# A cross-attention kernel: output rows on GpSimd, a two-operation end of the normalisation, weight folds from pieces, three loads on ScalarE's queue, new orders

## The chip, the cores and the metric

The kernel runs on one core of one Trainium2 chip. The metric is device time in microseconds (us), the median of several executions. The engines are TensorE (PE; PEld is its weight load), VectorE (DVE), ScalarE (ACT), GpSimd (POOL) and SyncE (SP), which here only issues transfers. Each engine works through its own instructions in order.

## What is computed

Sixteen batches (`B`), each with 100 query rows (`L`) and 361 context rows (`S`) of 512 features (`H`). A grouped attention layer with 32 query heads over 8 key heads of 16 features, residual and normalisation, and then a second, single-headed attention over the same context:

```python
q = hidden_state @ Wq + bq            # 32 heads, 4 per key head
k = encoder_hidden_state @ Wk + bk    # 8 heads
v = encoder_hidden_state @ Wv + bv
scores = jnp.einsum('bkgld,bksd->bkgls', q, k) * scale + mask
attn = jax.nn.softmax(scores, axis=-1)
out = jnp.einsum('bkgls,bksd->bkgld', attn, v)      # -> (B, L, H)
x = out @ Wo + bo + hidden_state
x1 = (x - mu) * jax.lax.rsqrt(var + EPS) * gamma + beta

q, k, v = x1 @ w_q.T, ctx @ w_k.T, ctx @ w_v.T
probs = jax.nn.softmax(q @ k.T / sqrt(512), axis=-1)
return x1 + alpha * (probs @ v) @ w_o.T
```

## The kernel before

Everything is fp32; products that need it are split in a high part (`_h`) and a low part (`_l`) and done as three fast products, in `product` (L505 to L507 of the profile). The second layer's four weights are folded once at the start into two 512x512 matrices, `fold_m` (w_q and w_k, 16 products, L669) and `fold_n` (w_v and w_o, L682).

A batch goes through these steps. Transposed x and context (`xT`, `cT`) are loaded and split: ScalarE writes the high part (`x_high`, `c_high`), GpSimd the low one (`x_low` L2333, `c_low` L2339). TensorE makes q, k and v. q and k go through DRAM (`queries_out`, `keys_out`, `stacks_in`) to be stacked, 96 rows deep. `heads` (L543) then makes the scores of each of the 32 heads once with the queries as rows; VectorE takes their row maxima (`maxima`, L1439). The maxima are turned, split (`maxima_high`, `maxima_low`) and written by `maxima_in` (L217) as rows 96 and 97 of the stack `qs`, for each half of the heads. `scores` (L526 for the first chunk of the keys, L530 and L531 for two more) makes the scores again, with keys as rows and the maxima subtracted. VectorE adds the mask to chunk 0 (L1425), ScalarE copies chunks 1 and 2 (`copy_scores`, L1912), GpSimd adds the mask there (`add_mask`, L2327), ScalarE takes the exponential (`probabilities`, L1918), TensorE multiplies by v (`values`, L559), each product with the sum of its row beside it.

Then comes the output path. `output` copies a half's rows to `o_s`, `rows_out` writes them to DRAM. `sums_in` (L232) and `rows_in` (L240) read back sums and rows; VectorE's `reciprocals` (L1477) inverts the sums; they go through DRAM (`reciprocals_out` L245, `reciprocals_in` L254) into `r_b`, spread over the rows. VectorE's `normalize` (L1482) multiplies, ScalarE's `o_high` (L2006) writes the high part, VectorE's `o_low` (L1486) the low one. `y_part` multiplies by Wo. `y_sum` adds the residual, to which GpSimd has added the bias (`residual_bias`, L2355); `y_stats`, `y_moments` (L1520) give mean and variance, GpSimd's `variance` and `deviation` (L2344, L2350) the reciprocal deviation, and VectorE ends the normalisation in three operations: `centre` (L1525, needs the deviation), `gain` (L1534), `shift` (L1539). `turn_x1` (L572) turns the result, and the second layer follows: `xm_part`, `turn_xm`, `s1_part` (L659), softmax, `turn_p1`, `cx_part` (L616), `d_part` (L626), `residual` (L1505), `result_out`. It needs the context twice more: `late_keys_in` (cT_s) and `ctx_in` (ctx_n).

The order of each engine's work is written out by hand, call by call: batches 0 to 3 and 12 to 15 singly, 4 to 12 by a loop over `i` on every engine. In turn `i`, TensorE does the later heads of batch `i` and the first of `i + 1`, the scores and values of `i - 1` and `i`, the q, k and v of `i + 1` and `i + 2`, and the second layer of `i - 2`, interleaved in small pieces. A wait stops all that its engine has behind it; that goes for SyncE's queue, which issues every transfer, too.

Of the kernel before, what the change touches and what calls it, by code (L numbers as in the profile page):

```python
# [14 lines left out]
P = 128  # L15
# [21 lines left out]
def build(nc, xT_d, x_d, ctxT_d, ctx_d, mask_d, maskT_d, wq_d, wk_d, wv_d, wo_d, bq_d, bk_d, bv_d,  # L37
          bo_d, gamma_d, beta_d, w1q_d, w1k_d, w1v_d, w1o_d, alpha_d, out_d):
    with ExitStack() as ctx:
# [3 lines left out]
        def sem(name):  # L43
# [71 lines left out]
        w_q, w_k, w_v, w_b, w_1, w_s, w_o, w_2 = (sem(n) for n in ("w_q", "w_k", "w_v", "w_b", "w_1", "w_s", "w_o", "w_2"))  # L115
        wh_ok, wl_ok, zero_ok, half_ok, bvb_ok = (sem(n) for n in ("wh_ok", "wl_ok", "zero_ok", "half_ok", "bvb_ok"))
# [19 lines left out]
        y_mm, y_ok, st_ok, mv_ok, ve_ok, rstd_ok, xc_ok, xg_ok, x1_ok = (  # L136
            sem(n) for n in ("y_mm", "y_ok", "st_ok", "mv_ok", "ve_ok", "rstd_ok", "xc_ok", "xg_ok", "x1_ok"))
# [10 lines left out]
        def _(sp):  # L148
# [26 lines left out]
            def weights_o():  # L175
                sp.wait_ge(wh_ok, 1)
                sp.wait_ge(wl_ok, 1)
                sp.dma_start(n_w[:, :, :].rearrange("p a b -> p (a b)"), wo_d).then_inc(w_o, 16)
# [9 lines left out]

            def ctx_turned_in(b):
                wait(sp, ch_ok, b)  # L190
                wait(sp, cl_ok, b)
                sp.dma_start(cT[:, :], ctxT_d[b, :, :]).then_inc(c_in, 16)
# [63 lines left out]
            def residual_in(b):  # L256
                wait(sp, xg_ok, b)
                sp.dma_start(y[:, :], x_d[b, :, :]).then_inc(xn_in, 16)

            def late_keys_in(b):  # L260
                if b == 0:
                    sp.wait_ge(g_mm, 4)
                wait(sp, l_mm, b)
                sp.dma_start(cT_s, ctxT_d[b, :, :]).then_inc(c4_in, 16)

            def ctx_in(b):
                if b == 0:
                    sp.wait_ge(g_mm, 4)
                wait(sp, cx_mm, b)
                sp.dma_start(ctx_n, ctx_d[b, :, :, :]).then_inc(cn_in, 16)  # L270
# [36 lines left out]
            fold_m_in()  # L307
            weights_v()
            weights_k()
            weights_q()  # L310
            mask_in(0)
            biases()
            x_turned_in(0)
            residual_in(0)
            mask_in(1)
            norm_in()
            ctx_turned_in(0)
            x_turned_in(1)
            weights_o()
            fold_n_in()  # L320
            queries_out(0)
            keys_out(0)
            ctx_turned_in(1)
            stacks_in(0, 0, 0, 2)
            stacks_in(0, 0, 2, 4)
            x_turned_in(2)
            stacks_in(0, 1, 0, 2)
            mask_turned_in(0)
            stacks_in(0, 1, 2, 4)
            mask_turned_in(1)  # L330
            queries_out(1)
            ctx_turned_in(2)
# [5 lines left out]
            x_turned_in(3)  # L338
# [3 lines left out]
            ctx_turned_in(3)  # L342
            rows_out(0, 0)
            queries_out(2)
            keys_out(2)
# [5 lines left out]
            x_turned_in(4)  # L351
            maxima_in(1, 1)
            rows_in(0)
            sums_in(0)
            mask_turned_in(2)
            stacks_in(2, 1, 2, 4)
            reciprocals_out(0)
            reciprocals_in(0)
            ctx_in(0)
            queries_out(3)  # L360
            rows_out(1, 0)
            maxima_in(2, 0)
            mask_in(3)
            keys_out(3)
            late_keys_in(0)
# [3 lines left out]
            ctx_turned_in(4)  # L369
            maxima_in(2, 1)  # L370
            rows_in(1)
            sums_in(1)
            x_turned_in(5)
            stacks_in(3, 1, 0, 2)
            reciprocals_out(1)
            residual_in(1)
            stacks_in(3, 1, 2, 4)
            mask_turned_in(3)
            reciprocals_in(1)
            rows_out(2, 0)  # L380
            mask_in(4)
            ctx_in(1)
            late_keys_in(1)
            queries_out(4)
            maxima_in(3, 0)
            keys_out(4)
            stacks_in(4, 0, 0, 2)
            stacks_in(4, 0, 2, 4)
            rows_out(2, 1)
            ctx_turned_in(5)  # L390
            result_out(0)
            maxima_in(3, 1)
            rows_in(2)
            sums_in(2)
            residual_in(2)

            for i in range(4, 13):
                stacks_in(i, 1, 0, 2)
                reciprocals_out(i - 2)
                stacks_in(i, 1, 2, 4)  # L400
                mask_turned_in(i)
                mask_in(i + 1)
                reciprocals_in(i - 2)
                late_keys_in(i - 2)
# [3 lines left out]
                x_turned_in(i + 2)  # L408
                rows_out(i - 1, 0)
                stacks_in(i + 1, 0, 0, 2)  # L410
                stacks_in(i + 1, 0, 2, 4)
                rows_out(i - 1, 1)
                ctx_turned_in(i + 2)
                sums_in(i - 1)
                ctx_in(i - 2)
                rows_in(i - 1)
                maxima_in(i, 1)
                residual_in(i - 1)
                result_out(i - 3)

            x_turned_in(15)
            reciprocals_out(11)
            late_keys_in(11)
            mask_turned_in(13)
            reciprocals_in(11)
            stacks_in(13, 1, 0, 2)
            stacks_in(13, 1, 2, 4)
            queries_out(14)
            ctx_turned_in(15)
            maxima_in(13, 0)  # L430
            keys_out(14)
            mask_in(14)
            rows_out(12, 0)
            stacks_in(14, 0, 0, 2)
            stacks_in(14, 0, 2, 4)
            rows_out(12, 1)
            stacks_in(14, 1, 0, 2)
            sums_in(12)
            maxima_in(13, 1)
            result_out(10)  # L440
            ctx_in(11)
            rows_in(12)
            reciprocals_out(12)
            residual_in(12)
# [2089 lines left out]
```

## Time and profile before

| what | value |
|---|---|
| median of 3 runs | 739.95 us (734.6 to 741.24) |
| the profiled execution, its own time | 737.84 us |
| its span | 736.1 us |
| TensorE busy | 669.4 us, 91% |
| VectorE busy | 512.7 us, 70% |
| ScalarE busy | 393.5 us, 53% |
| GpSimd busy | 369.4 us, 50% |
| mean granted TensorE clock | 0.972 |
| transfers | 110.51 MB, mean 150 GB/s |

The span is the time from first to last instruction in the profile, and some 1.7 us less than the time that is measured. A busy share of a matmul includes its pipeline, so TensorE at 91% is nearer its limit than the number says. The chain that ended last lies on TensorE for 49% of the span and on transfers for 23%. In the 40 slices of the page, TensorE is at 9 or 8 tenths from the second slice to the 35th.

### The profile page before, as it was taken

How to read it: one execution, taken by the hardware profiler on the slowest of the kernel's cores; microseconds unless marked ns; L12 is line 12 of the kernel's file. 1: busy time of each engine (PE TensorE's matmuls, PEld its weight loads, DVE VectorE, ACT ScalarE, POOL GpSimd, SP SyncE). 2: the span in 40 equal slices, each digit the busy share in tenths (PEclk: the TensorE clock that was granted, in tenths of full speed). 3: DMA queues.
4: the chain of work that ended last, by engine and by line, in shares of the span. 5: the costliest groups of instructions: out<-in, count | busy, mean ns of one | idle time of the engine just before them, and what ended most of it. 6: DMA issues, size and time to landing. Idle time of an engine off the chain costs nothing.

```text
span 736.1 us, 11738 instructions
## 1 busy us (share of the span) xinstructions
PE 669.4 (91%) x3658; PEld 462.2 (63%) x3658; DVE 512.7 (70%) x1467; ACT 393.5 (53%) x589; POOL 369.4 (50%) x225
## 2 busy tenths in 40 slices
PE   5998998989999999999989999999999989897756
PEld 2556656666676767776758677676767656563434
DVE  1258879778696869786857778696978778754120
ACT  2324766645566656666655656475666636564100
POOL 3454766545556564646455565556555534554000
PEclk9999999999999999999999999999999989999987
DMA  7696685755768685858493758678687644541500
GB/s 285 254 145 132 158 128 174 148 155 133 151 148 202 139 188 118 219 124 196 134 194 116 195 127 205 144 172 177 134 198 160 140 141 82 97 151 47 170 9 12
DMA packets 60856, 110.51 MB, mean 150 GB/s; under 512 B 11661, under 2 KB 50125, under 8 KB 60026
## 3 DMA queue, kind: packets, MB, share of 16 engines
q1 hardware_dynamic: 60794, 109.76, 63.2%
q8 instruction: 30, 0.49, 0.3%
q14 instruction: 32, 0.26, 0.2%
HBM read 86.79 MB, written 22.52 MB: 149 GB/s over the span
## 4 chain that ended last, share of the span: by engine, by line
PE 49%; DMA 23%; DVE 9%; issue 8%; SPq 7%; POOL 2%; ACT 1%; POOLq 0%; DVEq 0%; ACTq 0%
PE mx_ps L543 7%; PE work L505 6%; PE work L507 5%; PE work L506 5%; DMA qs<-mt_l 5%; PE work L626 5%; PE o_ps L559 5%; DMA late<-r_dr 4%; DMA r_dr<-rden 4%; DMA o_dr<-o_s 3%; PE work L616 3%; DMA k_dr<-k_l 3%; DVE mx_ps L1439 2%; DVE late L1482 2%; PE sc_ps L526 2%
## 5 line engine op out<-in xcount | busy, mean ns | idle before, releaser
L1439 DVE CUSTOM_DVE_ANT_0 mx_ps<-mx_ps,mask_n 100x361 f32<-100x361 f32 x512 | 270.2, 544 | 90.7 <-PE mx_ps L543 87.9
L2327 POOL TENSOR_TENSOR pr<-pr,mask_t 128x800 f32<-128x800 f32 x128 | 249.5, 1962 | 162.8 <-ACT pr L1912 162.6
L543 PE MATMUL mx_ps<-ks,qs 96*100 96x362 f32 x512 | 182.9, 379 | 12.9 <-DVE mx L1439 9.7
L1912 ACT ACTIVATE pr<-sc_ps 128x800 f32<-128x800 f32 x128 | 106.9, 835 | 106.1 <-PE sc_ps L531 59.7
L1918 ACT ACTIVATE pr<-pr 128x1200 f32<-128x1200 f32 x128 | 152.1, 1203 | 12.0 <-POOL pr L2327 7.2
L543 PEld LDWEIGHTS mx_ps<-ks,qs 96*100 96x100 f32 x512 | 85.2, 168 | 50.5 <-DVE mx L1439 25.8
L1425 DVE TENSOR_TENSOR pr<-sc_ps,mask_t 128x400 f32<-128x400 f32 x128 | 73.0, 571 | 17.5 <-PE sc_ps L526 10.6
L559 PE MATMUL o_ps<-pr,va 128*32 128x400 f32 (+1 forms) x768 | 72.7, 512 | 3.4 <-ACT pr L1918 3.4
L1439 DVE DVE_READ_ACCUMULATOR2_ANT mx<- 100x1 f32 x512 | 72.1, 141 | 0.0
L626 PE MATMUL work<-n_w,late 128*100 128x512 f32 x128 | 69.4, 635 | 1.5 <-ACT late L1984 1.4
L2339 POOL TENSOR_TENSOR c_l<-cT,c_h 128x1448 fp32r<-128x1448 f32 x16 | 53.6, 3350 | 29.7 <-ACT c_h L1939 29.7
L526 PE MATMUL sc_ps<-qs,ks 98*128 98x400 f32 x128 | 56.8, 444 | 11.1 <-DMA qs<-mt_l 10.9
L616 PEld LDWEIGHTS work<-late 128*128 128x128 f32 (+1 forms) x384 | 53.1, 199 | 3.9 <-ACT late L1979 1.6
L530 PE MATMUL sc_ps<-qs,ks 98*128 98x400 f32 x128 | 52.2, 408 | 3.1 <-ACT pr L1912 3.1
L616 PE MATMUL work<-late 128*128 128x100 f32 (+1 forms) x384 | 53.1, 281 | 1.3 <-ACT late L1979 1.3
L659 PE MATMUL work<-late 128*100 128x362 f32 x128 | 48.4, 469 | 1.5 <-ACT late L1965 1.4
L2355 POOL TENSOR_TENSOR y<-y,bo_b 100x512 f32<-100x512 f32 x16 | 20.5, 1280 | 55.7 <-DMA y<-in_x 55.7
L559 PEld LDWEIGHTS o_ps<-pr,va 128*32 128x32 f32 (+1 forms) x768 | 22.1, 111 | 39.8 <-issue 34.4
L531 PE MATMUL sc_ps<-qs,ks 98*128 98x400 f32 x128 | 44.1, 344 | 0.0
L526 PEld LDWEIGHTS sc_ps<-qs,ks 98*128 98x128 f32 x128 | 24.5, 192 | 25.9 <-DMA qs<-mt_l 15.6
L2344 POOL TENSOR_SCALAR ve<-mv 100x1 f32<-100x1 f32 x16 | 3.5, 221 | 63.8 <-DVE mv L1520 63.8
L1482 DVE TENSOR_TENSOR late<-o_l,late 128x400 f32<-128x400 f32 x16 | 24.2, 1510 | 13.3 <-DMA late<-r_dr 12.7
(121 smaller groups left out, 1149.3 us busy)
## 6 DMA issues: line engine op xcount, KB each, us to landing
qs<-q_dr SPq DMA_DIRECT2D x128, 100.0 KB, 4.8
late<-in_ctx SPq DMA_DIRECT2D x16, 768.0 KB, 4.7
cT<-in_ctxT SPq DMA_DIRECT2D x16, 724.0 KB, 5.9
ks<-k_dr SPq DMA_DIRECT2D x128, 90.5 KB, 4.4
late<-in_ctxT SPq DMA_DIRECT2D x16, 724.0 KB, 5.2
o_dr<-o_s SPq DMA_DIRECT2D x32, 200.0 KB, 3.7
xT<-in_xT SPq DMA_DIRECT2D x16, 200.0 KB, 3.2
y<-in_x SPq DMA_DIRECT2D x16, 200.0 KB
```

The costliest lines, as they stand in the source:

```text
L526: nc.tensor.matmul(sc_ps[:, 0, 0:JL], ks[p][:, g, 0:P], qs[p][:, g, :], start=True, stop=True).then_inc(s0_mm, 1)
L530: nc.tensor.matmul(sc_ps[:, 1, 0:JL], ks[p][:, g, P:2 * P], qs[p][:, g, :], start=True, stop=True)
L543: nc.tensor.matmul(mx_ps[0:L, n % 2, 0:SP2], qs[p][0:TERMS, g, L * j:L * (j + 1)], ks[p][0:TERMS, g, 0:SP2], start=True, stop=True).then_i ...
L559: mm = nc.tensor.matmul(o_ps[32 * q:32 * (q + 1), 0:JL], va[p][0:k, c, 4 * half + q, :], pr[0:k, q, c, :], start=(c == 0), stop=(c == SC - 1))
L616: mm = nc.tensor.matmul(work[:, 0, L * t:L * (t + 1)], ctx_n[0:k, c, P * t:P * (t + 1)], p1_t[0:k, c, :], start=(c == 0), stop=(c == SC - 1))
L626: mm = nc.tensor.matmul(work[0:L, 0, :], turned[:, L * k:L * (k + 1)], n_w[:, k, :], start=(k == 0), stop=(k == KT - 1))
L1425: V.tensor_tensor(pr[:, g % 4, 0, :].rearrange("p (j l) -> p j l", j=J), sc_ps[:, 0, 0:JL].rearrange("p (j l) -> p j l", j=J), mask_t[p][: ...
L1439: V.tensor_tensor_reduce(out=src, in0=src, in1=mask_n[p][:, :], scale=1.0, scalar=-3.0e38, op0=ALU.add, op1=ALU.max, accum_out=mx[p][:, n: ...
L1912: A.activation(pr[:, g % 4, 1:3, :], sc_ps[:, 1:3, 0:JL], ACT.Copy).then_inc(sc_cp, 1)
L1918: A.activation(t, t, ACT.Exp).then_inc(ex_ok, 1)
L2327: G.tensor_tensor(t, t, mask_t[p][:, 1:3, :].unsqueeze(2).to_broadcast([P, 2, J, L]), ALU.add).then_inc(sc_pool, 1)
L2339: G.tensor_tensor(c_l[:, :], cT[:, :], c_h[:, :].bitcast(F32), ALU.subtract).then_inc(cl_ok, 1)
```

## The change

Six things change, and the numbers of lines with them.

1. **Output rows.** `normalize` and `o_low` go from VectorE to GpSimd, the same operations on the same tiles. On GpSimd they stand between the mask additions of groups 5 and 6.
2. **The normalisation's end.** `centre`, `gain` and `shift` become two operations: (y - mean) * gamma, which no longer needs the deviation, and then times the deviation plus beta.
3. **Folds from pieces.** `fold_m`'s two matrices come as eight loads of 256 KB in place of two of 1 MB, with one semaphore for each pair; the fold's products wait for their piece only and are reordered. The splits of Wq, Wk and Wv have a semaphore each.
4. **Three loads on ScalarE's queue.** `ctx_turned_in`, `late_keys_in` and `ctx_in` (724, 724 and 768 KB for each batch) are issued by ScalarE in place of SyncE.
5. **`residual_in`** waits for `x1_ok` in place of `xg_ok`, which is gone, and `deviation` for `x1_ok` in place of `xc_ok`.
6. **New orders** on all five engines. The loop still covers 4 to 12.

```diff
-            def fold_m_in():
-                sp.dma_start(st[:, 0:2048], w1q_d).then_inc(w_1, 16)
-                sp.dma_start(st[:, 2048:4096], w1k_d).then_inc(w_1, 16)
+            def fold_m_in(o):
+                cs = slice(512 * o, 512 * (o + 1))
+                sp.dma_start(st[:, 512 * o:512 * (o + 1)], w1q_d[:, cs]).then_inc(w_1[o], 16)
+                sp.dma_start(st[:, 2048 + 512 * o:2048 + 512 * (o + 1)], w1k_d[:, cs]).then_inc(w_1[o], 16)
...
-            fold_m_in()
-            weights_v()
-            weights_k()
-            weights_q()
...
+            fold_m_in(0)
+            fold_m_in(1)
+            weights_q()
+            fold_m_in(2)
+            x_turned_in(0)
+            fold_m_in(3)
...
-            def centre(b):
-                dve.wait_ge(rstd_ok, b + 1)
-                dve.wait_ge(mv_ok, b + 1)
-                V.tensor_scalar(y[:, :], y[:, :], mv[:, 0:1], rstd[:, 0:1], ALU.subtract, ALU.mult).then_inc(xc_ok, 1)
...
-                V.tensor_tensor(x1[p][:, :], y[:, :], gamma_b[:, :], ALU.mult).then_inc(xg_ok, 1)
...
-                V.tensor_tensor(x1[p][:, :], x1[p][:, :], beta_b[:, :], ALU.add).then_inc(x1_ok, 1)
...
+                V.scalar_tensor_tensor(y[:, :], y[:, :], mv[:, 0:1], gamma_b[:, :], ALU.subtract, ALU.mult).then_inc(xc_ok, 1)
...
+                dve.wait_ge(xc_ok, b + 1)
+                dve.wait_ge(rstd_ok, b + 1)
...
+                V.scalar_tensor_tensor(x1[p][:, :], y[:, :], rstd[:, 0:1], beta_b[:, :], ALU.mult, ALU.add).then_inc(x1_ok, 1)
...
+            def ctx_turned_in(b):
+                wait(act, ch_ok, b)
+                wait(act, cl_ok, b)
+                act.dma_start(cT[:, :], ctxT_d[b, :, :]).then_inc(c_in, 16)
...
+            def normalize(b):
+                pool.wait_ge(ot_in, 16 * (b + 1))
+                pool.wait_ge(rb_in, 16 * (b + 1))
+                G.tensor_tensor(r_b, o_l[:, :].bitcast(F32), r_b, ALU.mult).then_inc(on_ok, 1)
+
+            def o_low(b):
+                pool.wait_ge(oh_ok, b + 1)
+                G.tensor_tensor(o_l[:, :], r_b, o_h[:, :].bitcast(F32), ALU.subtract).then_inc(ol_ok, 1)
```

Two places of the orders are shown. The first is GpSimd in one turn of the loop, before: `residual_bias` (writes y), `c_low` (writes c_l), the mask additions of the groups 4 to 7 (write pr), and the two small operations for the deviation.

```order
L2355 TENSOR_TENSOR y<-y,bo_b 100x512 [waits bo_ok,xn_in]
L2339 TENSOR_TENSOR c_l<-cT,c_h 128x1448 [waits v_mm,k_mm,ch_ok]
L2327 TENSOR_TENSOR pr<-pr,mask_t 128x800 [waits sc_cp] x4
L2344 TENSOR_SCALAR ve<-mv 100x1 [waits rstd_ok,mv_ok]
L2350 TENSOR_TENSOR rstd<-ve,half_c 100x1 [waits xc_ok,half_ok,ve_ok]
```

The same stretch of GpSimd after the change:

```order
L2338 TENSOR_TENSOR y<-y,bo_b 100x512 [waits bo_ok,xn_in]
L2313 TENSOR_TENSOR c_l<-cT,c_h 128x1448 [waits v_mm,k_mm,ch_ok]
L2301 TENSOR_TENSOR pr<-pr,mask_t 128x800 [waits sc_cp] x2
L2329 TENSOR_TENSOR late<-o_l,late 128x400 [waits rb_in,ot_in]
L2333 TENSOR_TENSOR o_l<-late,o_h 128x400 [waits oh_ok]
L2301 TENSOR_TENSOR pr<-pr,mask_t 128x800 [waits sc_cp] x2
L2318 TENSOR_SCALAR ve<-mv 100x1 [waits rstd_ok,mv_ok]
```

The multiplication by the reciprocals (late is the tile that holds r_b) and the low part, which waits for ScalarE's high part, now stand between groups 5 and 6.

The second is SyncE's queue where the maxima of the second half of a batch (mt_h, mt_l) go into the stack qs, before, with the rows of the output path (o_dr, den, o_l) and the context (cT, late) ahead of them:

```order
L224 DMA o_dr<-o_s 128x400 [waits dn_in,ot_in,os_ok1]
L192 DMA cT<-in_ctxT 128x1448 [waits cl_ok,ch_ok]
L232 DMA den<-o_dr 32x1x100 [waits rd_ok,os_out1,os_out0]
L270 DMA late<-in_ctx 128x1536 [waits cx_mm]
L240 DMA o_l<-o_dr 128x1x400 [waits y_mm,os_out1,os_out0]
L217 DMA qs<-mt_h 1x16x100 [waits ml_ok1,mh_ok1]
L217 DMA qs<-mt_l 1x16x100
```

The same place of SyncE's queue after the change:

```order
L222 DMA o_dr<-o_s 128x400 [waits dn_in,ot_in,os_ok1]
L201 DMA ks<-k_dr 16x4x362 [waits s0_mm,s12_mm,k_out,q_out]
L204 DMA qs<-q_dr 16x4x400
L201 DMA ks<-k_dr 16x4x362
L204 DMA qs<-q_dr 16x4x400
L215 DMA qs<-mt_h 1x16x100 [waits ml_ok1,mh_ok1]
L215 DMA qs<-mt_l 1x16x100
L230 DMA den<-o_dr 32x1x100 [waits rd_ok,os_out1,os_out0]
```

The maxima now go ahead of the load of den, which waits for the rows' way through DRAM, and the two context loads are no longer in this queue; half of the next batch's stack is ahead of them instead.

## Rows read from the trace of the kernel before

**Rows 1.** The page of the profile, busy time: us, share of the span, instructions.

```profile
PE 669.4 (91%) x3658; PEld 462.2 (63%) x3658; DVE 512.7 (70%) x1467; ACT 393.5 (53%) x589; POOL 369.4 (50%) x225
```

**Rows 2.** Stretches: length, busy us of each engine (instructions), granted clock, DMA, GB/s.

```profile
0.00:48.70 48.70, 38.92 (x113) 20.09 (x113) 10.92 (x14) 14.95 (x20) 19.43 (x18) 1.00 0.81 242
...
48.70:194.70 146.00, 134.83 (x740) 93.61 (x741) 120.26 (x359) 82.53 (x120) 85.99 (x48) 0.96 0.69 146
...
194.70:587.20 392.50, 379.42 (x2243) 274.85 (x2242) 307.89 (x908) 240.31 (x362) 217.57 (x131) 1.00 0.71 163
...
587.20:654.90 67.70, 59.87 (x319) 40.17 (x318) 53.97 (x151) 37.26 (x55) 34.74 (x21) 0.95 0.48 116
...
654.90:736.10 81.20, 56.38 (x249) 33.47 (x247) 19.65 (x37) 18.48 (x35) 11.63 (x10) 0.87 0.21 67
```

**Rows 3.** TensorE's waits, whole span: line, whom for, us, times, longest.

```profile
PE sc_ps L526 <- DMA qs<-mt_l: 10.9, 10, 2.6
...
PE mx_ps L543 <- DVE mx L1439: 9.7, 10, 4.5
...
PE sc_ps L669 <- DMA pr<-in_w1k: 8.2, 1, 8.2
...
PE work L572 <- DVE x L1539: 7.9, 4, 4.7
```

**Rows 4.** TensorE's waits in the stretch 194.7 to 587.2.

```profile
PE sc_ps L526 <- DMA qs<-mt_l: 10.6, 9, 2.6
```

**Rows 5.** Timeline, VectorE, GpSimd and TensorE from 585.6: start, length, instruction, idle before.

```profile
585.61 5.96 DVE L1482 TENSOR_TENSOR late<-o_l,late 128x400 f32<-128x400 f32 x1
...
585.98 3.33 POOL L2339 TENSOR_TENSOR c_l<-cT,c_h 128x1448 fp32r<-128x1448 f32 x1
...
589.21 1.94 POOL L2327 TENSOR_TENSOR pr<-pr,mask_t 128x800 f32<-128x800 f32 x1
...
592.14 0.62 PE L543 MATMUL mx_ps<-ks,qs 96*100 96x362 f32 x1 [4.45 <-DVE mx L1439]
```

**Rows 6.** Groups by line and form: busy us, mean ns, idle before and releaser.

```profile
L1482 DVE TENSOR_TENSOR late<-o_l,late 128x400 f32<-128x400 f32 x16 | 24.2, 1510 | 13.3 <-DMA late<-r_dr 12.7 <-DMA o_l<-o_dr 0.6
...
L1486 DVE TENSOR_TENSOR o_l<-late,o_h 128x400 fp32r<-128x400 f32 x16 | 10.4, 649 | 0.9 <-ACT o_h L2006 0.9
...
L1505 DVE SCALAR_TENSOR_TENSOR x<-work,ra,x 100x512 f32<-100x512 f32 x16 | 11.9, 747 | 22.1 <-PE work L626 22.0
...
L2333 POOL TENSOR_TENSOR x_l<-xT,x_h 128x400 fp32r<-128x400 f32 x16 | 16.8, 1051 | 19.9 <-ACT x_h L1933 15.5 <-issue 4.3
```

**Rows 7.** Timeline, SyncE's queue from 333.4 and the matmul behind it.

```profile
333.39 0.73 SPq L232 DMA_DIRECT2D den<-o_dr  x1
...
336.34 0.59 SPq L217 DMA_DIRECT2D qs<-mt_l  x1
...
341.47 0.45 PE L526 MATMUL sc_ps<-qs,ks 98*128 98x400 f32 x1 [1.00 <-DMA qs<-mt_l]
```

**Rows 8.** Timeline, GpSimd: two mask additions of one batch.

```profile
313.60 2.01 POOL L2327 TENSOR_TENSOR pr<-pr,mask_t 128x800 f32<-128x800 f32 x1 [0.66 <-ACT pr L1912]
319.48 1.94 POOL L2327 TENSOR_TENSOR pr<-pr,mask_t 128x800 f32<-128x800 f32 x1 [3.86 <-ACT pr L1912]
```

**Rows 9.** The start: a stretch of loading, and the first products.

```profile
4.00:6.00 2.00, 0.00 (x0) 0.00 (x0) 0.00 (x0) 0.00 (x0) 1.94 (x2) 1.00 1.00 414
...
8.19 13.32 PE L669 MATMUL sc_ps<-pr 128*128 128x512 f32 x24 [8.19 <-DMA pr<-in_w1k]
```

**Rows 10.** Timeline of the tail: VectorE and TensorE.

```profile
695.69 0.58 DVE L1482 TENSOR_TENSOR late<-o_l,late 128x400 f32<-128x400 f32 x1 [6.73 <-DMA late<-r_dr]
...
702.87 0.18 DVE L1520 BATCH_NORM_AGGREGATE mv<-stats 100x2 f32<-100x6 f32 x1
...
698.40 0.44 PE L505 MATMUL work<-wo_h,o_h 128*100 128x512 f32 x1 [0.93 <-DVE x L1505]
...
706.09 0.31 PE L572 MATMUL work<-ident,x 100*128 100x100 f32 x1 [4.72 <-DVE x L1539]
```

More of the change, by code:

```diff
@@ L1655, in _ @@
             y_moments(1)
-            maxima(3, 23, 25)
             centre(1)
-            gain(1)
+            maxima(3, 24, 25)
             shift(1)
-            add_mask(3, 0)
             maxima(3, 25, 27)
             x1_low(1)
+            add_mask(3, 0)
             maxima(3, 27, 29)
@@ L1804, in _ @@
             reciprocals(13)
-            maxima(15, 5, 9)
+            maxima(15, 4, 7)
             row_sum(12)
-            maxima(15, 9, 10)
+            maxima(15, 7, 8)
             add_mask(14, 4)
-            maxima(15, 10, 14)
+            maxima(15, 8, 14)
             add_mask(14, 5)
-            normalize(13)
             maxima(15, 14, 16)
+            residual(12)
             add_mask(14, 6)
-            residual(12)
-            o_low(13)
             maxima_low(15, 0)
-            maxima(15, 16, 19)
+            maxima(15, 16, 18)
             add_mask(14, 7)
-            maxima(15, 19, 20)
+            maxima(15, 18, 21)
             y_sum(13)
@@ L1841, in _ @@
             add_mask(15, 5)
+            residual(13)
             add_mask(15, 6)
-            normalize(14)
-            o_low(14)
-            residual(13)
             add_mask(15, 7)
@@ L1850, in _ @@
             centre(14)
-            gain(14)
             shift(14)
@@ L1855, in _ @@
             reciprocals(15)
-            normalize(15)
             row_sum(14)
-            o_low(15)
             residual(14)
@@ L1863, in _ @@
             centre(15)
-            gain(15)
             shift(15)
@@ L2375, in _ @@
             add_mask(0, 4)
-            residual_bias(0)
             add_mask(0, 5)
@@ L2385, in _ @@
             c_low(3)
+            residual_bias(0)
             add_mask(1, 4)
-            x_low(4)
             add_mask(1, 5)
+            normalize(0)
+            o_low(0)
             add_mask(1, 6)
@@ L2395, in _ @@
             add_mask(2, 2)
+            x_low(4)
             add_mask(2, 3)
             c_low(4)
+            normalize(1)
+            o_low(1)
+            add_mask(2, 4)
             residual_bias(1)
-            add_mask(2, 4)
             add_mask(2, 5)
@@ L2415, in _ @@
                 add_mask(i - 1, 5)
+                normalize(i - 2)
+                o_low(i - 2)
                 add_mask(i - 1, 6)
@@ L2419, in _ @@
                 deviation(i - 2)
-                add_mask(i, 0)
-                add_mask(i, 1)
-                add_mask(i, 2)
-                x_low(i + 2)
+            add_mask(12, 0)
+            add_mask(12, 1)
+            x_low(14)
+            add_mask(12, 2)
             add_mask(12, 3)
             c_low(14)
+            residual_bias(11)
             add_mask(12, 4)
             add_mask(12, 5)
+            normalize(11)
+            o_low(11)
             add_mask(12, 6)
             add_mask(12, 7)
-            residual_bias(11)
+            x_low(15)
             variance(11)
@@ L2435, in _ @@
             add_mask(13, 1)
-            x_low(15)
             add_mask(13, 2)
             add_mask(13, 3)
+            c_low(15)
+            normalize(12)
+            residual_bias(12)
             add_mask(13, 4)
-            residual_bias(12)
-            c_low(15)
             add_mask(13, 5)
+            o_low(12)
             add_mask(13, 6)
@@ L2451, in _ @@
             add_mask(14, 4)
+            residual_bias(13)
+            normalize(13)
+            o_low(13)
             add_mask(14, 5)
             add_mask(14, 6)
-            residual_bias(13)
             add_mask(14, 7)
@@ L2461, in _ @@
             add_mask(15, 3)
+            residual_bias(14)
             add_mask(15, 4)
+            normalize(14)
+            o_low(14)
             add_mask(15, 5)
-            residual_bias(14)
             add_mask(15, 6)
@@ L2468, in _ @@
             deviation(14)
+            normalize(15)
             residual_bias(15)
+            o_low(15)
             variance(15)
```

1403 lines of the change are left out of this document (692 added, 711 removed).

## The prediction

> **What bounds the kernel now.** I read the busy times first. TensorE is busy 91% of the span, VectorE 70%, GpSimd 50% [rows 1]. The table of stretches then tells stages apart [rows 2]. The middle, 194.7 to 587.2, holds ten batches, 39.25 us each, with 379.4 of 392.5 us busy on TensorE: only the 13.1 us of idle there, and slow clock, can be won. GpSimd is busy 217.6 us of it (21.8 in each batch), so it has room. The other stages have more idle: 9.8 us up to 48.7, 11.2 us from there to 194.7, 7.8 us from 587.2 to 654.9, and 24.8 us in the tail.
>
> TensorE's waits name the idle time [rows 3]. It waited 10.9 us in ten places at L526 for the maxima's transfer into qs, 10.6 of them in the middle [rows 4]; 9.7 us for VectorE's maxima; 8.2 us once for the first weights; 7.9 us for x1 from VectorE, most of it in the tail. So the middle is TensorE's own work plus one late small transfer, and the rest is VectorE being late at a few places.
>
> The timeline shows why the maxima came late at the worst of these [rows 5]. VectorE's `normalize` (L1482) took 5.96 us from 585.61. In that time GpSimd ran `c_low` (3.33 us) and an addition (1.94 us) without a gap, and TensorE stood idle 4.45 us for the next maximum. Over 16 batches `normalize` takes 1510 ns in the mean; `o_low`, of the same size, takes 649 [rows 6]. The Trainium skill (SBUF — State Buffer, "SBUF: two separate sides") says that a VectorE operation with two SBUF inputs and a GpSimd operation exclude each other for a whole instruction. By that rule the 5.96 us are a wait for GpSimd, and the trace agrees: the operation ends just behind GpSimd's last.
>
> **The change, part by part.** The sum is made against the profiled execution (737.84 us; 2.1 below the median).
>
> *Output rows.* VectorE loses 1.51 + 0.65 = 2.16 us a batch. GpSimd's nearest row is `x_low`, same size, 1051 ns [rows 6], so it gains 2.10 us: 21.8 becomes 23.9 of some 39. What hides it: between the mask additions of two neighbouring groups GpSimd idles up to 3.86 us, since ScalarE's next copy isn't there [rows 8]. The first addition shown starts at 313.60, the second at 319.48. Two operations ahead of the first, with the wait for ScalarE's `o_high` between (its engine is 61% busy, 240 of 392.5 us [rows 2]), push the first to about 316.5 and leave the second. So I cost it at nothing; uncovered it is 2.1 us plus that wait in every batch. What VectorE's being held has cost TensorE goes: of the 9.7 us for maxima I take 8 (the longest, 4.5, is this very case), and of the x1 waits outside the tail some 2: -10 us (bounds -5 and -12).
>
> *Three loads on ScalarE's queue, and the new place of the maxima.* Before, `maxima_in` of the second half stood behind the load of den, which started at 333.39 when the rows had come back from DRAM, and behind two context loads [rows 7]. Its issue came at 336.34, and the matmul waited until 341.47: about 5 us to land. Now nothing ahead of it waits for DRAM and the large loads are elsewhere. I take 8 of the 10.9 us (bounds -3 and -10.9). Three issues a batch cost ScalarE about 2 us, by SyncE's 0.59 and 0.73 us for one [rows 7] as the nearest price, next to some 15 us of idle a batch (240 busy of 392.5): nothing. The Trainium skill (DMA: Bandwidth & Descriptors, "Issuing engines are not separate DMA queues") speaks against a gain from the queue alone: transfers from all issuers run on the same engines, and another issuer only saves the time of issuing. By that rule only the new place counts. No run here shows it yet; I keep it as a rival.
>
> *Clock.* The granted clock was 0.96 over 146 us and 0.95 over 67.7 us [rows 2]: 5.8 + 3.4 = 9.2 us. The drops come in the stages with TensorE's longer waits, and the middle, without them, shows 1.00. With the waits mostly gone I take half back: -4.5 us (0 and -9.2).
>
> *Folds from pieces.* TensorE begins at 8.19, when 2 MB are there [rows 9]. At 414 GB/s 1.5 MB less take 3.7 us less; the first context load now shares the engines and takes part of it, up to 1.7 us for its 0.72 MB, so the first product starts about 5 to 5.5. After it TensorE is busy without a gap before (13.32 us for 24 records, two to a product: twelve of the 16 products, 1.1 us each), and later pieces come faster than that: 0.5 MB in 1.3 us feed four folds, 4.4 us. So the start moves with it, and the wait of 1.5 us for the first stacks (9.8 idle less 8.2) may go in part: -4 us (-2 and -5.5).
>
> *Tail.* From the moments (702.87 + 0.18) to `turn_x1` at 706.09 it is 3.0 us [rows 10]: deviation, then three operations. Now one of the three runs beside the deviation and one is gone. With 747 ns for the nearest such operation [rows 6] two in a row and the deviation partly beside them take 1.7 to 2.4 us: about -1 us in each of the last two batches. Against that, `y_part(15)` started at 698.40, while `normalize` could start at 695.69 and `o_low` ended about 697.4. On GpSimd the two take 2 x 1.05 in place of 2 x 0.58, and `residual_bias` stands between them: +1 us. Reading batch 14's rows ahead of its sums may give 1 us. Together -2 us (0 and -4).
>
> *New orders.* Every order that removes a wait makes others. Nothing in the trace prices that. At best 0; at worst the new orders wait as the middle does now, 13.1 us in ten batches, some 20 in all. I take a quarter, +5 us.
>
> Sum: -10 - 8 - 4.5 - 4 - 2 + 5 = -23.5 us. 737.84 becomes 714.3, the median of 739.95 about 716.
>
> **The rivals.**
>
> *A. The maxima stay late (0.16).* The small transfer runs on the same engines, busy 0.71 of the middle [rows 2], beside 400 KB of stacks and now a context load at the same time; or the orders find a new wait of the same size. Then 8 + half of the clock's 4.5 are not won, and new orders cost 8: the sum is -4 - 10 - 2 - 2.2 + 8 = -10: 730. For it: transfers are a hard limit no queue moves. Against: before, half of the delay was the queue's place, 333.39 to 336.34.
>
> *B. The covers fail, no change (0.12).* GpSimd's two operations push later additions, exponentials and `values` by 1 us in each of the 14 inner batches: +14 on the sum, with part of A: 735 to 745.
>
> *C. Slower (0.05).* GpSimd now waits, in its order, for `r_b` through DRAM; VectorE waited 12.7 us for it in 16 batches [rows 6]. All mask additions behind that wait stop, and TensorE's `values` with them. Past the cover of some 3 us the delay goes to TensorE whole. If `r_b` comes so late that each batch loses 2.5 us, 14 batches lose 35, against 23.5 won: 751. It decides from about 2.2 us a batch. Against: in the middle `normalize` mostly found its data.
>
> *D. Nearly all waits go (0.10).* The good ends of all parts: -5.5 - 10.9 - 12 - 9.2 - 4 = -41.6, with some left for new waits: 700 to 704.
>
> **Numbers.** Forecast 716 (705 to 726) has 0.57. The range reaches to A and toward D, 702 to 734, and leaves out B's and D's ends and C. A measurement of this kernel can tell about 1%, 7.4 us. Faster by more: the forecast, D, and most of A, 0.81. Within 1%: part of A and B, 0.13. Slower: C and the end of B, 0.06.
>
> **What would show it.** Right: TensorE's first product before 6 us; no L1482-like operation of VectorE over 1 us; the wait for qs<-mt_l under 3 us in all; the clock 1.00 from 194.7 on until the tail; the middle's batches under 38.5 us; GpSimd busy some 400 us with `normalize` near 1.05 us. Wrong: TensorE or ScalarE waiting for GpSimd's additions more than a few us; GpSimd waiting for late<-r_dr; transfers into qs still landing after 5 us. The forecast fails most easily in the middle: 1 us a batch is 14 us.

## The result: 5% slower

The changed kernel took 777.8 us in the median (774.5 to 779.4) where the kernel before took 740.6: a ratio of 1.051 (95% interval 1.044 to 1.058). The forecast was 716, with 702 to 734 as its range. Medians here and below are of all executions, ratios and their intervals of those within 1.5% of the fastest of their kernel, so the two need not agree to the last digit. The profiled execution has a span of 776.4 us, 40.3 above before.

The same five stretches as in [rows 2]. The first ends at 48.7 us in both kernels, the others at the same events (batch 5's and batch 15's q turned, the last maxima turned). Columns: length, busy us of each engine, granted clock, share of the transfer engines, GB/s.

```profile
0.00:48.70 48.70, 37.25 (x107) 18.93 (x107) 14.04 (x14) 15.05 (x20) 17.81 (x14) 0.99 0.88 249
48.70:201.80 153.10, 141.57 (x748) 97.83 (x749) 110.59 (x354) 82.32 (x120) 94.73 (x57) 0.91 0.60 135
201.80:643.90 442.10, 397.94 (x2238) 290.71 (x2237) 298.36 (x885) 237.03 (x359) 239.96 (x151) 0.93 0.62 146
643.90:703.50 59.60, 57.28 (x321) 38.86 (x320) 46.58 (x139) 38.83 (x56) 37.88 (x25) 1.00 0.51 130
703.50:776.40 72.90, 50.55 (x249) 29.53 (x247) 15.44 (x31) 18.44 (x35) 16.05 (x14) 0.94 0.22 71
```

The middle is 49.6 us longer (442.1 against 392.5), 5 us in each of its ten batches. The start up to batch 5 is 7.1 us longer: two waits for stacks (qs<-q_dr, 9.2 us for 2.6 before) and a clock of 0.91 for 0.96. The last two stretches are 8.1 and 8.3 us shorter. So the change does win time at the end, and loses much more in the middle. There TensorE's idle time went from 13.1 to 44.2 us, and its busy time, for the same work, from 379.4 to 397.9, since the clock fell from 1.00 to 0.93.

TensorE's waits over the whole span name the place: line, whom for, us, times, longest.

```profile
PE sc_ps L491 <- DVE pr L1393: 40.0, 10, 5.9
PE mx_ps L508 <- DMA qs<-q_dr: 9.5, 3, 6.5
PE work L537 <- DVE x L1494: 8.3, 10, 4.1
PE o_ps L633 <- DMA pr<-in_w1k: 7.1, 1, 7.1
PE sc_ps L495 <- DMA qs<-mt_l: 3.3, 2, 2.6
```

The wait that bounded the middle before (qs<-mt_l, 10.9 us in [rows 3]) is down to 4.6 with the 1.3 at L491, and the one for VectorE's maxima from 9.7 to 1.3. In their place stands a wait that before had 0.2 us: TensorE needs the score bank that VectorE's mask addition (L1393) reads. VectorE in its turn waited for a transfer:

```profile
DVE pr L1393 <- DMA mask_t<-in_maskT: 43.3, 9, 6.3
```

`mask_t` is the transposed mask, 150 KB for each batch. Nine times is once in every turn of the loop 4 to 12. GpSimd's mask additions waited for the same nine transfers (53.5 us). The timeline of one turn shows it, SyncE's and ScalarE's issues, then VectorE and TensorE (start, length, instruction, idle before):

```profile
390.13 0.33 ACTq L1870 DMA_DIRECT2D late<-in_ctxT  x1
390.56 0.71 ACTq L1864 DMA_DIRECT2D cT<-in_ctxT  x1
...
391.33 0.40 SPq L261 DMA_DIRECT2D mask_n<-in_mask  x1
391.83 0.84 SPq L267 DMA_DIRECT2D mask_t<-in_maskT  x1
396.61 0.33 SPq L201 DMA_DIRECT2D ks<-k_dr  x1
...
401.95 0.57 DVE L1393 TENSOR_TENSOR pr<-sc_ps,mask_t 128x400 f32<-128x400 f32 x1 [5.33 <-DMA mask_t<-in_maskT]
...
402.58 0.70 PE L491 MATMUL sc_ps<-qs,ks 98*128 98x400 f32 x1 [4.92 <-DVE pr L1393]
```

Two context loads of 724 KB go out on ScalarE's queue at 390.1 and 390.6. The mask follows at 391.8 and lands 10.1 us later. VectorE waits 5.3 us for it, TensorE 4.9. VectorE was ready for it at 396.6 (401.95 less 5.33), so the load had a lead of 4.8 us; in the nine turns it had 4.8 to 5.9. The kernel before issued the mask of this batch at 342.73 and used it at 366.44: 23.7 us ahead, and late landing did no harm. The stretches of 2 us show the transfer engines and the clock in this time:

```profile
395.00:397.00 2.00, 1.57 (x11) 1.26 (x12) 1.62 (x3) 1.06 (x2) 0.56 (x1) 1.00 1.04 419
397.00:399.00 2.00, 0.66 (x4) 0.32 (x2) 0.00 (x0) 1.51 (x3) 0.00 (x0) 1.00 0.92 221
399.00:401.00 2.00, 0.00 (x0) 0.00 (x0) 0.00 (x0) 0.00 (x0) 0.00 (x0) 0.68 1.11 129
401.00:403.00 2.00, 0.42 (x1) 0.42 (x2) 1.05 (x4) 0.00 (x0) 1.01 (x1) 0.50 1.12 134
403.00:405.00 2.00, 2.00 (x7) 1.79 (x7) 1.23 (x5) 0.48 (x2) 2.00 (x2) 0.50 1.10 173
405.00:407.00 2.00, 2.00 (x8) 1.67 (x7) 1.02 (x5) 1.18 (x2) 0.72 (x1) 0.62 0.97 110
407.00:409.00 2.00, 2.00 (x11) 1.52 (x10) 1.73 (x7) 1.84 (x2) 1.18 (x1) 1.00 0.66 161
```

The engines are full (share 0.9 to 1.1) from the context loads through the stacks that follow, and the idle time costs twice. The granted clock fell to 0.50 (1.2 GHz of 2.4) while TensorE stood idle and was 1.00 again at about 406.5 (the row from 405 has 0.62 in the mean), so TensorE worked at half its rate from 402.6 on for some 4 us. Nine such places at some 2 us lost make, as an estimate, the 18.5 us of added busy time.

### The profile page after: what moved, and what is told of

Read it like the earlier page. It is cut to its first block, busy times and chain, and to the rows that moved or that the text cites. A ratio compares the mean times of both kernels' runs of the same rounds, so it can differ in the third digit from the quotient of the medians.

```text
span 776.4 us, 11716 instructions
## 1 busy us (share of the span) xinstructions
PE 684.6 (88%) x3658; PEld 475.9 (61%) x3658; DVE 485.0 (62%) x1419; ACT 391.7 (50%) x589; POOL 406.4 (52%) x257
## 4 chain that ended last, share of the span: by engine, by line
PE 61%; DMA 21%; DVE 5%; issue 4%; POOL 4%; SPq 3%; ACT 2%; POOLq 0%; DVEq 0%; ACTq 0%
DMA mask_t<-in_maskT 12%; PE mx_ps L508 9%; PE work L591 6%; PE work L470 6%; PE work L471 6%; PE work L472 6%; PE work L581 5%; PE work L624 5%; PE o_ps L524 4%; PE sc_ps L491 3%; DMA qs<-q_dr 3%; PE sc_ps L495 2%; POOL pr L2301 2%; PE sc_ps L496 2%; DMA qs<-mt_l 2%
## 5 line engine op out<-in xcount | busy, mean ns | idle before, releaser
L2301 POOL TENSOR_TENSOR pr<-pr,mask_t 128x800 f32<-128x800 f32 x128 | 242.7, 1904 | 185.1 <-ACT pr L1843 131.5
L508 PE MATMUL mx_ps<-ks,qs 96*100 96x362 f32 x512 | 192.4, 396 | 11.2 <-DMA qs<-q_dr 9.5
L1849 ACT ACTIVATE pr<-pr 128x1200 f32<-128x1200 f32 x128 | 150.4, 1200 | 10.8 <-POOL pr L2301 7.2
L508 PEld LDWEIGHTS mx_ps<-ks,qs 96*100 96x100 f32 x512 | 89.5, 177 | 49.7 <-DVE mx L1407 15.8
L1393 DVE TENSOR_TENSOR pr<-sc_ps,mask_t 128x400 f32<-128x400 f32 x128 | 73.0, 571 | 62.5 <-DMA mask_t<-in_maskT 43.3
L491 PE MATMUL sc_ps<-qs,ks 98*128 98x400 f32 x128 | 56.3, 440 | 41.5 <-DVE pr L1393 40.0
L591 PE MATMUL work<-n_w,late 128*100 128x512 f32 x128 | 64.1, 593 | 1.5 <-ACT late L1932 1.4
L491 PEld LDWEIGHTS sc_ps<-qs,ks 98*128 98x128 f32 x128 | 25.5, 199 | 51.8 <-DVE pr L1393 43.7
L581 PEld LDWEIGHTS work<-late 128*128 128x128 f32 (+1 forms) x384 | 50.8, 191 | 3.7 <-ACT late L1927 1.8
L581 PE MATMUL work<-late 128*128 128x100 f32 (+1 forms) x384 | 50.9, 271 | 1.3 <-ACT late L1927 1.3
L2318 POOL TENSOR_SCALAR ve<-mv 100x1 f32<-100x1 f32 x16 | 7.5, 466 | 54.8 <-DVE mv L1480 54.8
L1949 ACT ACTIVATE vT<-work 128x362 f32<-128x362 f32 x16 | 7.5, 470 | 52.1 <-PE work L472 52.1
L470 PE MATMUL work<-m_h,x_h 128*100 128x512 f32 x64 | 30.4, 474 | 3.0 <-DVE x_l L1420 3.0
```

Source lines behind the costliest of these rows:

```text
L470: nc.tensor.matmul(dst, lh, rh, start=(k == 0), stop=False)
L491: nc.tensor.matmul(sc_ps[:, 0, 0:JL], ks[p][:, g, 0:P], qs[p][:, g, :], start=True, stop=True).then_inc(s0_mm, 1)
L508: nc.tensor.matmul(mx_ps[0:L, n % 2, 0:SP2], qs[p][0:TERMS, g, L * j:L * (j + 1)], ks[p][0:TERMS, g, 0:SP2], start=True, stop=True).then_i ...
L581: mm = nc.tensor.matmul(work[:, 0, L * t:L * (t + 1)], ctx_n[0:k, c, P * t:P * (t + 1)], p1_t[0:k, c, :], start=(c == 0), stop=(c == SC - 1))
L591: mm = nc.tensor.matmul(work[0:L, 0, :], turned[:, L * k:L * (k + 1)], n_w[:, k, :], start=(k == 0), stop=(k == KT - 1))
L1393: V.tensor_tensor(pr[:, g % 4, 0, :].rearrange("p (j l) -> p j l", j=J), sc_ps[:, 0, 0:JL].rearrange("p (j l) -> p j l", j=J), mask_t[p][: ...
```

## The experiments

Each kernel was compared with the kernel before on the same chip. The median of before was 737.4 beside e1 to e4, 738.1 beside e5 and e6, 739.0 beside e7, e7n, e8 and e9, and 738.1 beside e10 and e11.

### What made the mask late: its place, or the loads beside it?

**e1_mask_early**: the mask's load back in its old place.

```diff
                 stacks_in(i, 1, 2, 4)
+                mask_turned_in(i)
                 reciprocals_out(i - 2)
...
                 mask_in(i + 1)
-                mask_turned_in(i)
```

> The changed kernel with one line moved: in turns 4 to 12 the transposed mask of batch i is loaded right behind the fourth stack load, as in the kernel before, and no longer behind the keys, the result and the other mask. Theory (the place of this load costs the time): in the changed kernel VectorE waited 43.3 us in nine places for mask_t, TensorE 39.9 us behind it, and ran the middle at a clock of 0.93. The load's issue moves some 20 us ahead of its use, the waits fall under 2 us in all, the clock of the middle returns to 0.99 or 1.00, and the time is 777.8 - 40 - 10 to 18 for the clock = 720 to 730. Rival (the traffic of the large loads costs the time, whatever waits for it): the next transfer that is needed, stacks or maxima, becomes late in its place; half of the loss stays: 745 to 760.

**e2_quarter_loads**: everything in its place, but the two context loads a quarter of their size. This kernel leaves out three quarters of the context from batch 5 on (of the late load from batch 2 on) and computes with what an earlier batch left there, so its results are not the layer's.

```diff
-                act.dma_start(cT[:, :], ctxT_d[b, :, :]).then_inc(c_in, 16)
+                n = 1448 if b < 5 else 362
+                act.dma_start(cT[:, 0:n], ctxT_d[b, :, 0:n]).then_inc(c_in, 16)
...
```

> The changed kernel, all in its order, but from batch 5 on ctx_turned_in, and from batch 2 on late_keys_in, bring only the first 362 of 1448 columns (181 KB in place of 724 KB each); the rest of the tiles holds an earlier batch. If the mask is late because these two large loads, issued on ScalarE's queue 1 to 2 us ahead of it, keep the engines busy: its time to landing falls from 9.9 to 5 us or less, VectorE's waits for it from 43.3 to under 10 us in all, and the time to 725 to 745. If it is late by its place alone, or because of the stacks issued behind it: landing stays at 8 us or more, the waits at over 30 us, the time at 765 to 778.

**e4_before_mask_late**: the kernel before, its two mask loads moved to the late place.

```diff
-                mask_turned_in(i)
-                mask_in(i + 1)
                 reciprocals_in(i - 2)
...
                 keys_out(i + 1)
+                mask_in(i + 1)
+                mask_turned_in(i)
                 x_turned_in(i + 2)
```

> The kernel before with only the two mask loads of turns 4 to 12 moved to where the changed kernel has them, behind queries_out, maxima_in of the first half and keys_out; its large loads stay on SyncE's queue, away from this place. The load of mask_t is then issued some 6 us ahead of its use in place of 23.6. If the place alone does it, with a landing near the changed kernel's 9.9 us: 4 us a turn, 36 us in nine turns and some clock, 775 to 790. If it takes the large loads beside it to make it late: it lands in 4 to 6 us, under 1 us a turn is lost, 740 to 750.

e1 measured 762.0 (ratio 1.038, 1.025 to 1.050): my first theory, the place, gave 16 us of 40. e2 measured 738.9 (1.004, 0.998 to 1.010): nearly all of the 40, with the mask still in its late place; VectorE's waits for it fell from 43.3 to 15.0 us. Two signs were missed: the waits were to fall under 10 us and the landing to 5, but the mask still took 6.9 us in the median. In the same turn of e2 the mask goes out at 367.7, the stacks from 369.3 on, and the mask lands at 376.2, when five of these loads have landed: what the context loads hold back meets the stacks, and the two share the engines. How much of the delay is the stacks' no run takes apart. e4 measured 742.0 (1.006, 1.000 to 1.013): the late place alone costs the kernel before at most 1.3%, and there the mask, with a lead of 5.2 to 5.6 us, lands in 3.3 us, though the stacks follow it there too (at 363.9 and from 366.1 on): by themselves they don't make it late. The place takes the lead away; the traffic uses it up.

One execution of e1, the profiled one, took 1647.6 us, with matmuls about twice as long (775 ns at the heads, 379 in before); the other three took 760.3 to 763.2. So **e5_mask_early_again** is the kernel of e1 again, for its trace.

> The kernel of e1_mask_early once more, for its trace. It measured 762, 16 us less than the changed kernel and not the 40 to 58 that the theory of the place forecast. If the large loads' traffic is the cause, the trace shows VectorE's waits for mask_t gone, but some 15 to 25 us of TensorE's new waits for other transfers that land at the same time, qs<-q_dr or qs<-mt_l above all, and a clock below 0.96. If the place was all and something of the other orders costs the rest, TensorE's waits for transfers are under 8 us and those for VectorE, ScalarE or GpSimd are what is left.

763.7. TensorE's waits:

```profile
PE mx_ps L508 <- DMA qs<-q_dr: 38.8, 12, 6.2
PE work L537 <- DVE x L1494: 7.9, 9, 4.1
```

VectorE's wait for the mask is gone, and TensorE now waits 29.6 us in nine turns, at the first head of the next batch, for the stacks issued behind the same two loads. A wait was removed and the next late transfer took its place, as the rival of e1 said; the loss left was a little over that rival's range (745 to 760).

**e6_same_time_sp**: the changed kernel, the three large loads on SyncE's queue at the same moments.

```diff
                 x_turned_in(i + 2)
+                sp_ctx_in(i - 2)
                 queries_out(i + 1)
...
                 keys_out(i + 1)
+                sp_late_keys_in(i - 2)
+                sp_ctx_turned_in(i + 2)
                 result_out(i - 3)
```

> The changed kernel, but in turns 4 to 12 SyncE issues the three large loads, in the places of its queue that come at the moments at which ScalarE issued them: ctx_in behind x_turned_in(i + 2), late_keys_in and ctx_turned_in behind keys_out(i + 1), ahead of the result and the masks. If it is the moment of the loads that counts and not the queue: mask_t still lands 8 us or more after its issue and the time is 770 to 785. If the second queue itself slows SyncE's transfers by taking a share of the engines: the mask lands in order behind 1.45 MB at some 400 GB/s, in 4 to 5 us, and the time falls to 745 to 760.

779.8 (1.060, 1.046 to 1.074), against 777.8 with ScalarE as issuer; the mask lands in 9.3 us, VectorE waits 50.0 us for it. The queue made no difference here, the moment did. That is what the Trainium skill says (DMA: Bandwidth & Descriptors, "Issuing engines are not separate DMA queues"): another issuer only saves the time of issuing.

### Moving the two loads

**e7n_spread_only** is the changed kernel with the two loads at another moment of the turn; **e7_loads_spread** has the mask's early place too.

```diff
             for i in range(4, 13):
+                late_keys_in(i - 2)
+                ctx_turned_in(i + 2)
                 q_high(i + 1)
...
                 x_high(i + 2)
-                late_keys_in(i - 2)
-                ctx_turned_in(i + 2)
```

> The changed kernel with only these two loads moved, the mask's load left at its late place, issued some 10 us ahead of its use. Theory (traffic): it lands in 4 to 6 us, VectorE's waits for mask_t fall from 43.3 to under 10 us in all, and the time is within 8 us of e7_loads_spread. Rival (place and traffic both count): the mask stays 2 us or more late in each of nine turns, and the time is 15 us or more above e7_loads_spread.

> The kernel of e1_mask_early with late_keys_in(i - 2) and ctx_turned_in(i + 2) moved from behind x_high(i + 2) to the start of ScalarE's turn i, some 14 us earlier, into a stretch in which the trace of e5 shows the transfer engines at a share of 0 to 0.3. Theory (the traffic beside the urgent transfers costs the time): TensorE's 38.8 us for qs<-q_dr fall to the 9 us of the start, and the time from 762 by 30 us and some clock to 720 to 730. Rival (the rest of the changed orders costs it): 745 or more, with another wait of TensorE of over 15 us in the middle.

e7n measured 717.6 (0.972, 0.962 to 0.981), e7 711.8 (0.972, 0.965 to 0.979). Two lines moved turn 5% slower into 3% faster, more than the 720 to 730 that was expected of e7. The page of e7, busy times, and its middle stretch:

```profile
PE 662.7 (94%) x3658; PEld 461.0 (65%) x3658; DVE 483.3 (68%) x1419; ACT 391.1 (55%) x589; POOL 406.9 (58%) x257
...
192.10:570.70 378.60, 374.54 (x2238) 274.18 (x2237) 296.89 (x884) 235.92 (x359) 239.59 (x150) 1.00 0.71 170
```

In e7n the mask is issued only 5.8 us ahead of its use (399.6 and 405.4), as late as ever, and lands in 3.6. VectorE waits for it 0.2 us in all. So the changed kernel, e4 and e7n issue the mask equally late, and its median landing is 9.9, 3.3 and 3.6 us.

**e11_before_loads_late** puts that neighbourhood into the kernel before.

```diff
                 keys_out(i + 1)
+                late_keys_in(i - 2)
+                ctx_turned_in(i + 2)
+                mask_in(i + 1)
+                mask_turned_in(i)
                 x_turned_in(i + 2)
```

> The kernel before with late_keys_in(i - 2) and ctx_turned_in(i + 2) put right ahead of the two masks at their late place (as in e4), behind keys_out(i + 1): the neighbourhood that the changed kernel has, with nothing else of the change. Theory (the large loads ahead of the urgent small ones are the cause): mask_t lands in 8 to 10 us in place of e4's 3.3, VectorE waits for it 2 to 5 us a turn, and what is behind it, the stacks, is late too: 760 to 790. Rival (it takes more of the changed orders): the landing stays under 6 us and the time within 8 us of e4's 742.

783.3 (783.6, 783.0, 790.6 and 770.3, too far apart for a ratio with an interval). With nothing else of the change, the loss is there: 41 us above e4 by the medians, and the fastest execution is 16 us above the slowest of e4's ten (754.3). The mask lands in 7.6 us in the execution of 783.6, VectorE waits 30.3 us for it, and the maxima behind it on VectorE hold TensorE:

```profile
DVE pr L1425 <- DMA mask_t<-in_maskT: 30.3, 9, 4.4
...
PE mx_ps L543 <- DVE mx L1439: 35.3, 20, 4.5
```

So the neighbourhood is sufficient, and e7 shows that without it the rest of the change is a gain.

### The prediction's steps, on the orders of before

**e3_before_norm_pool**: `normalize` and `o_low` on GpSimd behind `add_mask(b + 1, 5)`, nothing else.

```diff
                 add_mask(i - 1, 5)
+                normalize(i - 2)
+                o_low(i - 2)
                 add_mask(i - 1, 6)
```

> The kernel before with one part of the change: normalize and o_low on GpSimd, between the mask additions of groups 5 and 6, nothing else moved. The prediction's step says -10 us (bounds -5 and -12): no VectorE operation held for several us, TensorE's waits for maxima from 9.7 to under 2 us: 728 to 735. Rival: GpSimd's later additions are pushed by the two operations and hold ScalarE's exponentials and the products with v by about 1 us a batch: +5 to +14, 745 to 755.

**e8_before_ctx_moved**: one load, one place.

```diff
                 late_keys_in(i - 2)
                 queries_out(i + 1)
+                ctx_in(i - 2)
...
                 sums_in(i - 1)
-                ctx_in(i - 2)
                 rows_in(i - 1)
                 maxima_in(i, 1)
```

> The kernel before with one move: ctx_in(i - 2), 768 KB, from right ahead of maxima_in of the second half to behind queries_out(i + 1), some 20 us earlier, where the trace of before shows the transfer engines nearly idle. In before the maxima were issued 0.9 us after VectorE had written them, in 29 of 32 places, and landed some 5 us later, so their place in the queue cost nothing. If the traffic of ctx_in makes them late: TensorE's 10.6 us for qs<-mt_l in the middle fall under 4 us and the time by 5 to 10 us, to 728 to 733 against some 738. If the stacks and cT ahead of them do it: 8 us or more of these waits stay, and the time is within 3 us of before.

**e9_norm_and_ctx**: both.

> e3_before_norm_pool and e8_before_ctx_moved together: two steps of the prediction (VectorE's held operations gone, -10; the maxima in time, -8) on the orders of before. In e3 TensorE's waits for maxima from VectorE went, but those for qs<-mt_l rose from 10.9 to 18.3 us. If both steps add up: 715 to 725. If GpSimd's two operations only exchange one wait for another: within 4 us of e8.

| kernel | us | ratio to before, 95% |
|---|---|---|
| e3, output rows on GpSimd | 732.7 | 0.989 (0.966 to 1.012) |
| e8, ctx_in moved | 720.2 | 0.983 (0.977 to 0.989) |
| e9, both | 712.3 | 0.969 (0.962 to 0.977) |

e3 alone is within what can be measured. Its trace has no wait for VectorE's maxima in the middle any more (1.4 us before), but the next wait, that of [rows 4], grew from 10.6 us:

```profile
PE sc_ps L526 <- DMA qs<-mt_l: 18.3, 9, 5.5
...
185.80:587.80 402.00, 383.68 (x2243) 276.58 (x2242) 293.95 (x890) 240.07 (x362) 237.51 (x151) 0.98 0.70 160
```

Between the same events as in [rows 2] the middle of e3 takes 402.0 us, 9.5 more than before; what e3 wins it wins ahead of it (185.8 us for 194.7) and behind it (145.7 for 148.9).

With `ctx_in` out of the way (e8) this wait is not there at all. The time to landing of the 32 transfers of `mt_l` (shortest, median, longest), in before and in e8:

```profile
DMA to landing us min/median/max: 1.8/1.9/6.5
...
DMA to landing us min/median/max: 1.8/1.8/3.4
```

In the nine turns of the loop the second half's maxima took 4.4 to 6.5 us to land in before, and 1.8 to 2.8 in e8. The gain was larger than expected (728 to 733). VectorE's held operations show as what bounds next, in the middle of e8 and, longest, just behind it:

```profile
PE mx_ps L543 <- DVE mx L1439: 2.7, 2, 2.2
...
580.40 0.62 PE L543 MATMUL mx_ps<-ks,qs 96*100 96x362 f32 x1 [4.44 <-DVE mx L1439]
```

e9 takes both away, and its middle has TensorE busy in all of its 374.3 us, 37.4 a batch:

```profile
189.90:564.20 374.30, 374.30 (x2243) 275.38 (x2241) 293.77 (x890) 240.07 (x362) 237.40 (x151) 1.00 0.73 171
```

On top of e8, the output rows on GpSimd are worth 8 us by the medians, near the step's 10. The intervals of the two ratios just touch; of the six executions of each, four of e9 (707.5 to 714.0) lie below all of e8 (715.8 to 724.8), two (718.5 and 720.7) do not. The middle of e9 is 9.3 us shorter than e8's 383.6.

**e10_norm_ctx_two_op** adds the normalisation's end in two operations.

> e9_norm_and_ctx with the normalisation's end in two operations, residual_in and deviation waiting for x1_ok. The prediction's step says -1 us in each of the last two batches; the changed kernel's trace shows 4.1 us for the last wait of turn_x1 in place of 4.7. Expected if the operations are all that changes: TensorE's waits for x1 in the tail from 5.9 to 4.5 to 5.2 us and a time within 3 us of e9's 712. Rival: residual_in now waits for the last operation and comes later, and deviation waits for the batch before to be finished, so that y or rstd are late in the middle: 716 or more.

713.3 (0.967, 0.959 to 0.976), the same as e9. TensorE's waits for x1 in the tail fell from 5.9 to 4.1 us. TensorE has no wait at all in the middle, so the rival falls. The gain is too small to be seen in the time.

## Why the prediction was wrong

**What bounds.** Right as to the places: the late maxima were most of the middle's idle time, VectorE's held operations came next once these were gone (e8), and with both gone (e9) no idle time is left there. Wrong as to what stood behind the maxima, see below.

**Output rows: -10 us.** About right: 8 us of e9 against e8, and in the changed kernel the wait for maxima fell by 8.4. GpSimd's two operations took 1043 and 1037 ns, for 1051 assumed, and TensorE waited only 0.9 us in all for an exponential. So the mechanisms of rivals B and C fall: `normalize` waited 25.6 us for `r_b` in five places, only 4.6 of them in the middle, and no wait of TensorE leads back to it. That C's side of zero came out is no credit to C.

**Three loads and the place of the maxima: -8 us. This is the step that failed**, in two ways. First, I read the delay of the maxima as half the queue's, "333.39 to 336.34". But VectorE began to write `mt_l` only at 335.01. In before its issue came 0.9 to 1.5 us behind that start in all 32 places, with the issue of `mt_h` in between; the queue had cost next to nothing. The delay was the landing, 5 us, beside `ctx_in`'s 768 KB, and e8 shows that by moving only this load. These waits did fall by 6.3 us in the changed kernel, near the term's 8, but because `ctx_in` had left that moment, not because the den load had left the queue ahead of them: as far as the queue goes, that was luck. Second, I priced the three loads by their issue on ScalarE, "nothing", and did not ask at which moment they now start and what starts beside them. In the changed kernel two of them go out back to back just ahead of the mask and the first stacks of the next batch. Of the mask, whose lead had gone from 23.7 us to about 5, the prediction says nothing at all: I had followed the queue only around the maxima. Price, where the prediction had nothing: 40 us of idle time, and the slower clock behind it.

Rival A named the mechanism, "transfers are a hard limit no queue moves", but priced it as a gain not made (730), for the maxima. It was the mask and the stacks, small things needed at once, and the price was a loss on the far side of zero. The rival that I did put on that side hung on another transfer, `r_b`.

**Clock: -4.5 us.** The sign followed the waits: with 31 us more idle time in the middle the clock cost 18.5 us more there. In e7 and e9 it is 1.00 in the middle, as forecast. The term left out the last stretch, which had the lowest clock of all in [rows 2] (0.87); it was 0.94 in the changed kernel and 0.89 in e7.

**Folds: -4 us.** The first product began at 7.11, not at 5 to 5.5: 1.1 us earlier than the 8.19 of [rows 9]. The wait is still for w1k's first piece. And then the first heads waited 6.5 us for their stacks, which before had cost 1.5: the start was spent on the next transfer, and the first heads began at 50.9 us, where before they began at 48.7 (in e7n at 48.8, in e7 at 46.1).

**Tail: -2 us.** The moments end at 748.46 and `turn_x1` comes at 750.88: 2.4 us where [rows 10] have 3.0. The step said 1 us a batch; it is 0.6. The last two stretches won 16.4 us in all: 8.4 in TensorE's busy time (57.28 + 50.55 against 59.87 + 56.38, at a higher clock) and 8.0 in idle time, 4.5 of them the one held `normalize` of [rows 5].

**New orders: +5 us.** The term was there for what I couldn't see, but its worst case, 20 us, was taken from the waits that existed. A transfer that loses its lead beside a burst isn't held to that: it cost 40. One smaller wait that the orders made also stands in e7: 3.0 us in the middle for VectorE beside GpSimd's `x_low` (last section).

With the burst gone the time is near the forecast: 716, and e7n and e7 measured 717.6 and 711.8. That the sum comes out is in part luck, since of the folds' 4 us the first heads show nothing in e7n (48.8 us for 48.7) and 2.5 us in e7, and the two last stretches of e7 won 12.0 us (58.8 and 78.1 us long, before 67.7 and 81.2), where the tail's 2, the held `normalize` of 4.5 and half of that clock's 3.4 make 8.2.

## What to carry to other kernels

When a change moves loads, list for every small transfer that something needs soon the time from issue to use, before and after, and what large loads start in the microseconds ahead of it, on any queue. In this kernel the small transfer issued 1 to 2 us behind two large ones landed behind both, from either queue (e6). Give the large loads, which have slack, the moments at which the transfer engines idle. And before a late transfer is put down to its queue, compare the issue with the moment at which its source was written.

## What the runs showed of the hardware

Full engines don't mean many bytes. In the changed kernel the engines' share was 1.04 at 419 GB/s during the context loads, and 1.11 at 129 GB/s during the stacks of `ks` and `qs`. In e7, where no large load is under way beside them, the stacks show the same:

```profile
359.00:361.00 2.00, 1.72 (x12) 1.71 (x13) 2.00 (x7) 1.12 (x3) 1.89 (x1) 1.00 1.08 151
```

Half a batch's stacks, eight loads of 762 KB together, keep the engines busy longer than a context load of about the same size, so megabytes don't tell what a transfer costs its neighbours.

VectorE's last operation of the normalisation (L1494) has two lengths for the same shape. Eight of its sixteen took 749 to 752 ns. The other eight, all of the loop's turns, began 0.1 to 0.2 us behind the start of GpSimd's `x_low`, took 1407 to 1475 ns and ended 0.55 us behind the end of `x_low`; e7 shows the same eight times. The turn shown above, and then the same operation in e10 (L1526 there; shortest, median, longest ns), whose order has no operation of GpSimd at its start:

```profile
394.52 1.04 POOL L2307 TENSOR_TENSOR x_l<-xT,x_h 128x400 fp32r<-128x400 f32 x1
394.64 1.48 DVE L1494 SCALAR_TENSOR_TENSOR x<-y,rstd,beta_b 100x512 f32<-100x512 f32 x1 [0.51 <-DVE y L1486]
...
L1526 DVE SCALAR_TENSOR_TENSOR x<-y,rstd,beta_b x16: 751/752/755, 125.7 to 684.6; 100x512 f32<-100x512 f32 x16
```

So the operation is held until `x_low` is through, as `normalize` was in [rows 5]. Of the 4.1 us that TensorE still idles in the middle of e7, 3.0 are this wait:

```profile
PE work L537 <- DVE x L1494: 3.0, 7, 0.4
```

One thing stays open. The start is the same code in e2, e5, e6, e7n and e7 as in the changed kernel, yet the first heads' wait for their stacks was 3.5, 6.2, 3.8, 4.8 and 0.7 us, against 6.5. So the start varies by some 6 us between executions of one code; a part of e7's lead over e7n is this, and nothing here says why it is so.
